# Folding the key mask into K and V in phase one of a cross-attention kernel, with the score maximum and difference taken from PSUM on VectorE and the split of x moved to GpSimd

## The reference

```python
qh = _split_heads(q @ wq.T + bq, h)
kh = _split_heads(k @ wk.T + bk, h)
vh = _split_heads(v @ wv.T + bv, h)
scores = jnp.einsum('ntd,nsd->nts', qh, kh) / jnp.sqrt(depth)
km = jnp.repeat(mask.astype(scores.dtype), h, axis=0)[:, None, :]
scores = scores + km * PAD                      # PAD = -2**32 + 1
attn = jax.nn.softmax(scores, axis=-1)
out = _merge_heads(jnp.einsum('nts,nsd->ntd', attn, vh), h) + q
mu = jnp.mean(out, axis=-1, keepdims=True)
var = jnp.var(out, axis=-1, keepdims=True)
out = (out - mu) / jnp.sqrt(var + LN_EPS) * gamma + beta
```

## Time and profile before

| | |
|---|---|
| median of 3 runs | 1162.73 us (1161.62 to 1169.27) |
| the profiled execution | 1162.73 us; 1161.0 us from its first to its last instruction |
| mean granted TensorE clock | 0.991 |
| PE busy | 1121.1 us (97%) |
| DVE busy | 929.3 us (80%) |
| POOL busy | 853.3 us (74%) |
| ACT busy | 609.7 us (53%) |

### The profile page before, as it was taken

One profiled execution on the slowest core, in us unless ns is written; L12 is line 12 of the kernel. 1 busy time (PEld: TensorE's weight loads), 2 busy tenths in 40 slices (PEclk: granted clock), 3 DMA queues, 4 the chain that ended last, 5 costly groups with the idle time before them and its releaser, 6 DMA issues.

```text
span 1161.0 us, 26005 instructions
## 1 busy us (share of the span) xinstructions
PE 1121.1 (97%) x7536; PEld 1036.0 (89%) x7536; DVE 929.3 (80%) x1677; ACT 609.7 (53%) x1003; POOL 853.3 (74%) x711
## 2 busy tenths in 40 slices
PE   7999799999999999999999999999999999999993
PEld 7888699999989899999999998998999999989983
DVE  5233568888888888888889888888888888888787
ACT  5221355556555655555555565665555555655551
POOL 1310235888878788888888887888888888878886
PEclk9999899999999999999999999999999999999997
DMA  7756233333333444443343333444433334334323
GB/s 246 276 187 240 67 90 89 90 107 105 109 117 113 125 125 125 125 115 107 90 122 122 97 115 115 118 125 125 125 116 113 102 104 124 102 107 119 88 78 132
DMA packets 147399, 142.00 MB, mean 122 GB/s; under 512 B 86917, under 2 KB 87941, under 8 KB 147365
## 3 DMA queue, kind: packets, MB, share of 16 engines
q1 hardware_dynamic: 147364, 141.56, 40.4%
HBM read 92.65 MB, written 48.85 MB: 122 GB/s over the span
## 4 chain that ended last, share of the span: by engine, by line
POOL 43%; issue 23%; PE 16%; DVE 4%; POOLq 1%; DMA 1%; SPq 1%; ACT 0%; DVEq 0%; ACTq 0%
POOL probs L905 12%; POOL y L881 11%; POOL attn L873 9%; POOL y L884 8%; PE q_ps L618 6%; PE o_ps L659 4%; PE s_ps L634 3%; PE t_ps L645 2%; POOL rstd L889 2%; DMA xT_raw<-in_xT 1%; DVE probs L793 1%; POOLq L903 0%; DVE stats L724 0%; DVE row_max L801 0%; POOL shift L891 0%
## 5 line engine op out<-in xcount | busy, mean ns | idle before, releaser
L905 POOL TENSOR_TENSOR probs<-probs,row_max 128x616 f32<-128x616 f32 x255 | 310.9, 1219 | 178.2 <-DVE row_max L801 178.1
L937 ACT ACTIVATE probs<-probs 128x616 f32<-128x616 f32 x256 | 183.4, 716 | 324.0 <-POOL probs L905 322.0
L659 PE MATMUL o_ps<-v_tiles,pt 128*128 128x66 f32 x2520 | 310.6, 270 | 2.6 <-DVE attn L716 2.6
L659 PEld LDWEIGHTS o_ps<-v_tiles,pt 128*128 128x128 f32 x2520 | 304.0, 192 | 3.1 <-issue 3.1
L793 DVE TENSOR_TENSOR probs<-s_ps,mask_pad 128x616 f32<-128x616 f32 x256 | 202.6, 792 | 49.0 <-PE s_ps L634 48.8
L618 PE MATMUL q_ps<-x_lo,wq_hi 128*128 128x512 f32 x500 | 218.2, 436 | 8.4 <-DVE q_lo L783 6.3
L801 DVE TENSOR_REDUCE row_max<-probs 128x8 f32<-128x616 f32 x256 | 202.3, 790 | 12.1
L618 PE MATMUL q_ps<-x_hi,wq_lo 128*128 128x512 f32 x500 | 197.8, 396 | 0.0
L618 PE MATMUL q_ps<-x_hi,wq_hi 128*128 128x512 f32 x500 | 197.3, 395 | 0.0
L884 POOL TENSOR_TENSOR y<-y,beta_all 128x512 f32<-128x512 f32 x123 | 177.1, 1440 | 9.6
L777 DVE TENSOR_TENSOR x_lo<-xT_raw,x_hi 128x512 fp32r<-128x512 f32 x124 | 148.5, 1200 | 40.4 <-ACT x_hi L947 40.4
(11 more groups left out here) (86 smaller groups left out, 1461.4 us busy)
## 6 DMA issues: line engine op xcount, KB each, us to landing
xT_raw<-in_xT SPq DMA_DIRECT2D x32, 1024.0 KB, 5.5
x_rows<-in_x SPq DMA_DIRECT2D x32, 1024.0 KB, 5.8
out<-y SPq DMA_DIRECT2D x128, 256.0 KB, 2.1
k_scratch<-k_out SPq DMA_DIRECT2D x8, 1232.0 KB, 5.4
bd_hi<-k_scratch SPq DMA_DIRECT2D x128, 38.5 KB, 1.8
bd_lo<-k_scratch SPq DMA_DIRECT2D x128, 38.5 KB, 1.8
v_scratch<-v_out SPq DMA_DIRECT2D x16, 264.0 KB
v_tiles<-v_scratch SPq DMA_DIRECT2D x256, 9.9 KB
```

The source lines that it names most:

```text
L659: mm = pe.matmul(bank_of(b, t)[:, col:col + tile_cols[i]], pt[h][0:w, i, P * t:P * t + P], v_tiles[v_buffer(b, h)][0:w, i, 0:tile_cols[i]] ...
L905: pool.tensor_tensor(v, v, row_max[:, u, :].unsqueeze(2).broadcast_to([P, HH, S]), ALU.subtract).then_inc(shifted, 1)
L937: act.activation(probs[h][:, t, :], probs[h][:, t, :], ACT.Exp).then_inc(exp_done, 1)
```

## The change

It has three parts.

1. **The mask moves into phase one.** K is masked (`keep` is 1 for a kept key and 0 for a masked one), centred on the mean of the kept keys of its batch and head, and masked again, so that a masked row is zero; V and its column of ones are multiplied by `keep`. For this DVE makes `k_part` (L384), its sums (L389) and the negative means (L392) and later the low part (L401); POOL adds the mean (L282) and multiplies by `keep` (L286); ACT copies the high part. POOL multiplies each V tile by `keep_v` (L298). The mask comes in through five small DMAs near the start, and PE turns it into rows by five transposes between the first two halves of keys. `k_ps[m]` is now free at `k_masked`, after DVE's first operation, and a bank of `v_ps` at `v_biased`.
2. **Phase two has no mask addition.** DVE takes the maximum straight from the scores in PSUM (L883) and writes scores minus maximum to `probs` (L892) in the same step. POOL subtracts nothing, and PE's scores wait for `shifted`.
3. **The split of x** goes from DVE to POOL, at the same steps `s` = 3 to 6.

```diff
 # SP, phase one
                 sp.dma_start(bk_col[:], bk).then_inc(bk_loaded, DMA)
+                for q in range(HG):
+                    sp.dma_start(keep[DH * q:DH * q + DH, :, :, :].bitcast(I32).rearrange("p g i s -> p g (i s)"),
+                                 mask_heads[q].partition_broadcast(DH)).then_inc(mask_loaded, DMA)
                 sp.dma_start(ctx_raw[:, :, HR:CR], ctx_src[:, :, 0, HR:CR]).then_inc(ctx_loaded, DMA)
+                sp.dma_start(keep_h[:].bitcast(I32), mask
+                             ).then_inc(mask_loaded, DMA)
 # POOL, phase one
+                def centre_keys(c, half):
+                    for m in range(NG):
+                        n = (2 * c + half) * NG + m
+                        part = k_part[:, n % KS, :, :, :]
+                        pool.wait_ge(k_mean_ready, n + 1)
+                        pool.tensor_tensor(part, part,
+                                           neg_mean_k[:, n % KS, :, :].unsqueeze(3).broadcast_to([P, HB // 2, 2, S]),
+                                           ALU.add).then_inc(k_centred, 1)
+                        pool.wait_ge(k_centred, n + 1)
+                        pool.tensor_tensor(part.rearrange("p c i s -> p c (i s)"),
+                                           part.rearrange("p c i s -> p c (i s)"), keep_of(m), ALU.mult).then_inc(k_ready, 1)
+                for c in range(CHUNKS):
+                    centre_keys(c, 0)
+                    centre_keys(c, 1)
+                    keep_values(c)
+                    if c == 0:
+                        pool.wait_ge(wq_hi_ready, 1)
+                        pool.tensor_tensor(wq_lo[:], w_raw[:], wq_hi[:], ALU.subtract).then_inc(wq_lo_ready, 1)
+                    if c == 1:
+                        pool.wait_ge(x_hi_ready, KC)
+                        for k in range(KC):
+                            pool.tensor_tensor(x_lo0[:, k, :], xT_raw[:, k, :], x_hi0[:, k, :], ALU.subtract
+                                               ).then_inc(x_lo_ready, 1)
 # DVE, phase one
+                def keys(c, half):
+                    first = (2 * c + half) * NG
                     for m in range(NG):
+                        centre_of_keys(first + m)
+                        if m >= 2:
+                            low_keys_out(first + m - 2)
+                    for m in range(NG - 2, NG):
+                        low_keys_out(first + m)
...
+                dve.wait_ge(count_step, 3)
+                keys(0, 0)
                 dve.wait_ge(wv_hi_ready, 1)
                 dve.tensor_tensor(wv_lo[:], w_raw[:], wv_hi[:], ALU.subtract).then_inc(wv_lo_ready, 1)
 # PE, phase one
+                pe.wait_ge(rows_step, 3)
+                for j in range(VT):
+                    mm = pe.transpose(v_ps[3][0:v_n[j], HEADS * j:HEADS * j + HEADS],
...
-                            pe.wait_ge(k_copied, (2 * c + half - 1) * NG + m + 1)
+                            pe.wait_ge(k_masked, (2 * c + half - 1) * NG + m + 1)
...
-                        at_least(pe, v_copied, c * VT + j - 3)
+                        at_least(pe, v_biased, c * VT + j - 3)
 # DVE, phase two
+                        if real(a):
+                            subtract_max(a, h, t)
 # POOL, phase two
+                        if 3 <= s <= 6 and real(a + 2):
+                            split_x(a + 2, s - 3, par)
```

More of the change, by code:

```diff
@@ L29, in xattn @@
     B, T, D = x.shape
-    S = mask.shape[1] // HEADS
+    S = mask.shape[2]
     DH = D // HEADS
@@ L47, in xattn @@
     HR = HB * S
+    KS = 4
     VT = -(-CR // P)
@@ L83, in xattn @@
         ident = sb(whole, "ident", [P, P], F32)
-        mask_pad = [sb(whole, f"mask_pad{i}", [P, HEADS * S], F32) for i in range(2)]
         xT_raw = sb(whole, "xT_raw", [P, KC, T], F32)
@@ L209, in _ @@
                 sp.dma_start(beta_all[:], beta.partition_broadcast(P)).then_inc(consts_loaded, DMA)
-                for i in range(2):
-                    sp.dma_start(mask_pad[i][:].bitcast(I32), mask[i].partition_broadcast(P)).then_inc(mask_loaded, DMA)
                 for c in range(CHUNKS):
@@ L292, in _ @@
                     if c == 0:
+                        act.wait_ge(keep_turned, 1)
+                        for j in range(VT):
+                            act.copy(keep_v[0:v_n[j], j, :], v_ps[3][0:v_n[j], HEADS * j:HEADS * j + HEADS]
+                                     ).then_inc(keep_v_ready, 1)
                         act.wait_ge(wv_loaded, DMA)
@@ L392, in _ @@
                         key_products(0, 0, m, k)
+                pe.wait_ge(ident_set, 1)
+                pe.wait_ge(rows_step, 3)
+                for j in range(VT):
+                    mm = pe.transpose(v_ps[3][0:v_n[j], HEADS * j:HEADS * j + HEADS],
+                                      keep_rows[:].rearrange("h c i s -> h (c i s)")[:, P * j:P * j + v_n[j]],
+                                      ident[0:HEADS, 0:HEADS])
+                mm.then_inc(keep_turned, 1)
                 for c in range(CHUNKS):
@@ L420, in _ @@
                 pe.wait_ge(x_lo_ready, KC)
-                pe.wait_ge(k_copied, 2 * NG * CHUNKS)
+                pe.wait_ge(k_masked, 2 * NG * CHUNKS)
                 for g in range(2):
@@ L435, in xattn @@
         scores_done = sem("scores_done")
-        masked = sem("masked")
         max_ready = sem("max_ready")
@@ L628, in scores @@
                     pe.wait_ge(k_loaded[par], b * (KDMA // 2) + (KDMA - par * (KDMA // 2)))
-                    at_least(pe, masked, b * 8 + (4 * h + t - 1))
+                    at_least(pe, shifted, b * 8 + (4 * h + t - 1))
                     for j in range(2):
```

179 lines of the change are left out of this document (103 added, 76 removed).

## The result

The changed kernel takes **1200.3 us** (median of 4 runs, 1196.4 to 1201.7) and the kernel before 1163.97 on the same chip (4 runs, 1161.62 to 1169.27): ratio 1.0316, 95% interval 1.029 to 1.0341. The profiled execution of the changed kernel took 1196.4 us, with a span of 1194.6.

What follows compares the result with a forecast made beforehand. PE was taken to bound both phases. Phase one's +45.3 us and -7.5 for the rest gave +37.8 on the profiled 1162.73, so 1200.5 us, with a range from 1181 to 1219.

Steps and rivals of the forecast that it cites:

- start, `keep_rows`: At the start PE, there at 14.71, waits for the mask's rows and goes on at 19.9: +5.2 us.
- `wv_lo`: Before the first values, the value weights' low part comes at 32.6, where PE needs it at 26.8: +5.8 us.
- chunk 1: V's first bank is free 37.9 us after the chunk's first key product; PE asks at 24.7: +13.1 us.
- chunk 2: V's first bank is free 38.3 us after the chunk's first key product; PE asks at 24.7: +13.5 us.
- contention: Phase one: DVE's low parts and POOL's pairs delay each other, 0.5 us a half, six halves: +3 us (0 to +9).
- clock: Phase one: PE's lower granted clock after four long waits, two losses half hidden: +4 us (0 to +8).
- `q_lo` waits: Phase two: with x_lo off DVE, five PE waits shrink to about zero: -6.0 us (-6.3 to -3).
- main term: Chunks 1 and 2: later key copies delay the next context's load and the value banks: +13.1 and +13.5 us.
- C: Chunks 1 and 2: PE's four value banks still cover everything, only phase two's gains stay: 1155 us; chance 0.04.
- A: Phase one: POOL and DVE delay each other more, a pair costs 2.2 us, not 1.6: about 1216; chance 0.17.
- B: Phase one: context 3 us sooner in each chunk, no clock loss, mask 2 us earlier: 1185; chance 0.16.
- D: Start costs 5 + 5 us, chunks nothing; gains and losses meet within 1% of 1162.7; chance 0.03.

Runs made afterwards that it cites:

- The order of the splits: Changed kernel with DVE's context split moved behind the third value tile and ACT's behind the second key half, load left late: 1173.82 us, ratio 1.0105.
- the early load: Changed kernel with SP's load of the context of chunks 2 and 3 put ahead of the key store: 1181.05 us, ratio 1.0165.
- the first experiment: Phase one of the kernel before, mask loaded but not used, with the changed kernel's phase two: 1155.11 us, ratio 0.9939 to the kernel before.
- the last kernel: Changed kernel with load, chunk and start reordered, `wq_lo` in chunk 2, no drain between key halves, chunk 1's splits earlier: 1157.63 us, ratio 0.9963 to the kernel before.
- the runs with the other start: Changed kernel with maskings and both value-weight splits earlier, mask transposes later: 1201.62 us with that alone; later runs combine it with other edits.

## Why the prediction was right

The forecast of 1200.5 us met 1200.3, and the steps can be held against the trace one by one. That it met the median to 0.2 us is luck: it was counted from 1162.73, where the median of the kernel before is now 1163.97, so the rise was 36.3 us by the medians and 33.7 between the profiled executions (1196.4 is the fastest of the four), for 37.8 forecast. The last column is from the profiled executions.

| step of the prediction | said | measured |
|---|---|---|
| start, `keep_rows` | +5.2 | +3.9 |
| `wv_lo` | +5.8 | +3.2 |
| first value bank, chunk 0 | +0.7 | 0 |
| chunk 1 | +13.1 | +13.8 |
| chunk 2 | +13.5 | +14.2 |
| contention | +3 | in the rows above (0.7 in chunk 1, 0.7 in chunk 2) |
| clock | +4 | +9.6, all that is no wait; about 8 of it clock |
| **phase one** | **+45.3** | **+44.6** |
| where phase two begins | +1.0 | +0.8 (5.3 for 4.53) |
| `q_lo` waits | -6.0 | -5.9 (0.4 for 6.3) |
| the end | -2.5 | -1.4 (PE's waits 4.7 for 6.1) |

**The main term held, mechanism and size.** I had counted from PE's first key product of chunk 1: POOL takes up the keys at 7.7, `k_copied` at 15.0, DVE's next key operation 13.65 later, the bank free at 37.9. In the trace PE began chunk 1 at 48.11, and the steps are 6.8 (54.93), 14.9 (63.02), 13.7 (76.71) and 38.6 (86.72). A pair on POOL took 1.66 to 1.86 us for the 1.6 taken. PE's idle stretches lay where the prediction had them, from 15.6, 29.5, 73.0 and 116.2 us on.

The order of the splits and the early load, each alone, removed that term, so it is shown and not only read. One word of the prediction was too narrow: it put the delay down to the load behind the store. With the load left there and the split moved, the term is gone all the same (1173.82 us).

**Two sizes were wrong and cancelled.** The waits came to 35.0 us where the prediction had 38.3 and 3 for contention. What is no wait was 9.6 where it had 4 for the clock, about 8 of it clock, which is the bound that it gave. They belong together. Behind the wait of 3.85 us PE worked more slowly: from 20.01 to 32.69, less the wait of 3.16, it needed 9.5 us for keys that took 6.87 before. Each such microsecond comes off the next wait, because what PE waits for arrives by another engine's clock. I had priced the losses one at a time and called two of them half hidden; the better price is the delay of PE's borders. Counted so, the start was right: its two terms are such delays, 5.2 + 5.8 = 11.0, and the first value product began 11.1 us later than before, at 32.69 for a forecast of 32.6. Chunk 0's values then took 1.5 us more, chunks 1 and 2 15.7 and 16.4 us, for 0.7, 13.1 and 13.5 before the surcharges.

**Contention met another instruction.** The prediction named the low parts as what POOL would hold; they took 0.48 us at the median and 0.79 at most, against the 0.47 taken. The small product of the mean, priced at 0.17, took 0.55 at the median and 3.76 and 4.03 us at the chunk borders. That cost PE next to nothing, since POOL's pairs set the pace: with the product on ScalarE the four pairs of chunk 1 took 6.7 us instead of 7.0, and the time did not fall. None of the low parts was held for a whole pass, which the prediction had priced at about 8 us.

**One gain had the wrong reason.** The prediction gave the 6.0 us of `q_lo` waits to x_lo's leaving DVE. With x_lo back on DVE these waits stayed at 0.4 us. The gain belongs to the second part, the maximum and difference from PSUM and the differences that leave POOL, together. The Trainium skill, page "SBUF — State Buffer", section "Who interferes with whom", says that DVE instructions with two SBUF inputs contend with GpSimd instructions that read SBUF, and that DVE with at most one SBUF input, outside its two-port modes, does not. (Its words "for the whole instruction", which the prediction cites, stand there in the sentence on DVE's two-port modes, and the maximum has no SBUF input at all, not one.) This case agrees: x_lo's mean on DVE fell from 1230 to 921 ns when POOL's differences went.

**Phase two as a whole.** From the last matmul on `k_ps` to the last of all it took 1011.5 us in the profiled execution of the changed kernel for 1022.4 before, so 10.9 less, and 8.1 less in that of the first experiment. The three rows of the table are 6.5 of them. In the even course four batches took 125.2 us each time in the changed kernel, and 125.1 to 128.0 before. The granted clock accounts for part of the rest. Behind the wait where phase two begins it was 0.50 for 4.9 us before and for 2.8 us in the changed kernel, and near the end it was 0.50 from 1135.9 to 1139.3 us before and nowhere in PE's last batches in the changed kernel. At half speed that is an estimated 1.0 and up to 1.7 us. The first experiment, which gained less, had both stretches (4.9 and 3.3 us at 0.50). The 1 to 2 us still missing stay open. The wait where phase two begins was 3.6 to 5.4 us in the runs that share the changed phase two, so the match of that row (+0.8 for +1.0) is luck.

**The rivals.** C, that four banks cover everything, fell as argued: idle time ahead of `ctx_lo` did not help what stood behind it. A needed pairs of 2.2 us, and they took up to 1.86. B needed the context to land 3 us sooner; from issue to ACT's split it took 8.25 us, for 8.20 before. (The last 3 us of its sum the prediction does not explain; they equal its term for contention.) D needed both chunk waits to be nothing.

## What to carry to other kernels

On an engine that works in order, place an instruction that waits for a transfer behind all work whose inputs are already there. Here that one placement was worth 24 to 26 us, and in the last kernel all the added arithmetic costs phase one 2. When a wait is removed, ask at once what is due next on the same engine: 7.0 us of waits at the start went, and 9.3 came back in the following stage until that place was mended too. And before you price an instruction that looks held up, look whether its consumer would have been free.

## What the runs showed of the hardware

- A product of 128x4 elements on VectorE with both inputs in SBUF took 0.16 us alone and 3.76 us next to GpSimd's `wq_lo`, 4.03 us next to its x split; it ended within 0.02 us of them. The x split is four GpSimd instructions of 1.28 us, and the product came 1.0 us into the first, so it was held over three borders between them. The maskings that read PSUM and the sums next to it stayed at 0.54 and 0.47 us. The size of an instruction gives it no protection.
- VectorE's `tensor_scalar` of 128x8 elements took 1.20 us in the changed kernel, from 15.83 us, beside two GpSimd memsets of 1.12 us that ended at 15.93 and 16.99, and 0.15 us when the memset had ended, in the runs with the other start.
- A low split of 128x2464 elements took 2.7 us alone and 3.55 to 3.61 us next to GpSimd's masking of the values.
- ScalarE needs 0.24 us for each of two products of 128x2 elements with a pointer scale, so a tiny step costs more there than the 0.16 us on an undisturbed VectorE.
- TensorE's granted clock fell to its lower level (1.2 of 2.4 GHz) during each of the four waits of the changed kernel and stayed there for a while behind it: 0.50 from 20 to 24 us, 0.54 from 32.7 to 36, 0.50 from 86.7 to 90 and from 130.4 to 134. The third wait in windows (columns as above); PE had been idle since 73.0 us and began again at 86.72:

```profile
74.00:76.00 2.00, 0.00 (x0) 0.00 (x0) 1.93 (x1) 0.04 (x1) 0.00 (x0) 1.00 0.00 0
78.00:86.00 8.00, 0.00 (x0) 0.00 (x0) 6.39 (x14) 2.31 (x6) 6.37 (x8) 0.50 0.00 0
86.70:90.00 3.30, 3.27 (x8) 2.32 (x9) 1.76 (x3) 0.86 (x2) 3.25 (x4) 0.50 0.93 346
90.40:92.00 1.60, 1.60 (x11) 1.36 (x10) 0.57 (x1) 0.00 (x0) 0.42 (x1) 1.00 0.84 147
```

  Behind the waits of 3.9, 3.2, 13.8 and 14.2 us PE worked at the lower level for 6.1, 3.0, 3.6 and 4.3 us, so a longer wait did not bring a longer slow stretch. Together the four cost about 8 us on 35.0 us of waits.
